# A routed expert layer: token table and gathers instead of scattered slots, and four result planes instead of two with accumulation

## The reference

```
logits = x2 @ gate_w.T
probs = jax.nn.softmax(logits, axis=-1)
top_w, top_i = jax.lax.top_k(probs, TOPK)           # 4 of 16 experts
top_w = top_w / jnp.sum(top_w, axis=-1, keepdims=True)
wfull = jnp.sum(jax.nn.one_hot(top_i, E, dtype=x2.dtype) * top_w[..., None], axis=1)
gu = jnp.einsum('th,eih->tei', x2, w1)              # 2 x 176 per expert
act = jax.nn.silu(g) * u
down = jnp.einsum('tei,ehi->teh', act, w2)
routed = jnp.einsum('te,teh->th', wfull, down)
shared = jax.nn.silu(sg) * su @ sh_down_w.T         # a dense expert of 352
return hid + (routed + shared).reshape(b, s, h)
```

## Time and profile before

| what | value |
|---|---|
| median of 3 runs | 1990.88 us (1988.37 to 1996.01) |
| the profiled execution's own time | 1989.11 us |
| its span in the profile | 1987.3 us |
| mean granted TensorE clock | 0.922 of full speed |
| busy share: PE, weight loads, DVE, ACT, POOL | 87%, 73%, 59%, 48%, 27% |
| `sort_and_share` | from 1609 us to 1756 us |
| `routed_experts`, first tile's load to last scatter landed | 1756 us to 1966 us |
| planes, adds, store | 1966 us to 1987 us |

### The profile page before, as it was taken

One profiled execution on the slowest core, in us unless ns is written; L12 is line 12 of the kernel. 1 busy time (PEld: TensorE's weight loads), 2 busy tenths in 40 slices (PEclk: granted clock), 3 DMA queues, 4 the chain that ended last, 5 costly groups with the idle time before them and its releaser, 6 DMA issues. The chain is left out here.

```text
span 1987.3 us, 34326 instructions
## 1 busy us (share of the span) xinstructions
PE 1722.4 (87%) x11668; PEld 1455.4 (73%) x11668; DVE 1165.0 (59%) x2625; ACT 951.5 (48%) x2452; POOL 529.5 (27%) x527
## 2 busy tenths in 40 slices
PE   7998897697699999999992999999999969259993
PEld 6666664555688888888881788888888867258883
DVE  4688884698655656566546555555555457335553
ACT  2577776486355444545541444444454423225442
POOL 4133321243311111111111111111121114736663
PEclk7699997898899999999996999999999968679997
DMA  4111121265100100100002101001000043447666
GB/s 142 55 34 29 29 70 40 78 252 213 43 13 1 43 12 13 43 1 11 1 1 77 43 1 32 12 12 29 5 12 1 1 117 108 147 101 139 126 115 162
DMA packets 73274, 117.40 MB, mean 59 GB/s; under 512 B 8285, under 2 KB 59021, under 8 KB 71943
## 3 DMA queue, kind: packets, MB, share of 16 engines
q1 hardware_dynamic: 54014, 89.03, 14.4%
q0 software_dynamic: 14448, 19.80, 5.6%
q10 hardware_dynamic: 4648, 6.38, 1.0%
HBM read 86.65 MB, written 44.70 MB: 66 GB/s over the span
## 5 line engine op out<-in xcount | busy, mean ns | idle before, releaser
L1812 ACT ACTIVATE da_prob<-da_prob,da_nb,d_rqs 128x128 f32<-128x128 f32 x256 | 123.3, 483 | 260.2 <-DVE da_nb L2072 260.2
L1812 ACT ACTIVATE hold_wq<-hold_wq,ca_nb,c_rqs 128x128 f32<-128x128 f32 x256 | 123.4, 483 | 235.4 <-DVE ca_nb L2072 235.4
L653 DVE TENSOR_REDUCE a_mx<-a_s 128x2 f32<-128x512 f32 x256 | 167.1, 681 | 60.5 <-PE a_s L541 58.7
L470 ACT ACTIVATE a_prob<-a_s 128x512 f32<-128x512 f32 x256 | 147.4, 600 | 85.7 <-PE a_s L554 85.4
L1874 POOL TENSOR_TENSOR hold_wq<-hold_wq,ca_rsum 128x512 f32<-128x512 f32 x64 | 66.7, 1042 | 428.3 <-DVE ca_rsum L2077 428.3
L1874 POOL TENSOR_TENSOR da_prob<-da_prob,da_rsum 128x512 f32<-128x512 f32 x64 | 66.6, 1041 | 422.9 <-DVE da_rsum L2077 422.9
L2700 POOL DMA_INDIRECT slot_results<-t_ysb,t_dest x79 | 124.3, 1574 | 91.7 <-ACT t_ysb L2714 42.8
L554 PE MATMUL a_s<-a_qs,a_ks 32*128 32x256 f32 x512 | 101.6, 346 | 32.4 <-ACT a_prob L470 32.3
L1884 PE MATMUL da_qk<-d_xTh,da_wqkv_h 128*128 128x512 f32 x256 | 106.7, 417 | 6.4 <-DVE da_wqkv_l L2023 6.4
L541 PE MATMUL a_s<-a_ks,a_qs 32*128 32x256 f32 x512 | 101.0, 351 | 3.1 <-DVE a_mx L653 3.0
L2084 DVE SCALAR_TENSOR_TENSOR ca_oT_l<-ca_oT,ca_bv,ca_oT_h 128x512 fp32r<-128x512 f32 x64 | 48.0, 751 | 93.3 <-ACT ca_oT_h L1826 93.3
(11 more groups left out here) (412 smaller groups left out, 5610.2 us busy)
## 6 DMA issues: line engine op xcount, KB each, us to landing
t_xg<-slot_rows SPq DMA_DIRECT2D x79, 144.0 KB, 2.5
mw_raw<-in_d_expert_w SPq DMA_DIRECT2D x16, 352.0 KB, 6.1
slot_results<-in_d_fill SPq DMA_DIRECT2D x1, 4608.0 KB
a_heads<-a_osb SPq DMA_DIRECT2D x128, 32.0 KB
a_wraw<-a_heads SPq DMA_DIRECT2D x32, 128.0 KB, 2.1
mw_down<-in_d_expert_d SPq DMA_DIRECT2D x1, 2816.0 KB
hold_wk<-in_c_wkT SPq DMA_DIRECT2D x1, 2064.0 KB
hold_wq<-in_c_wqT SPq DMA_DIRECT2D x1, 2064.0 KB, 9.0
```

The lines of the kernel that those rows point to most:

```text
L470: act.activation(prob[:, w % PR, :, :], s2[w % 2][:, :, :], ACT.Exp, scale=1.0 / A_ROOT)\
L653: dve.tensor_reduce(mx[:, b % 2, :, h], s1[s1_use(b, u) % S1_BANKS][:, :, :], AX.X, ALU.max)\
L1812: ins = act.activation(prob[:, p, b, :], prob[:, p, b, :], ACT.Exp, bias=nb[:, p, b:b + 1], scale=rqs[:, r:r + 1], accum_out=sums[:, p, b: ...
```

## The change

The slots are no longer filled by scattering rows. The 2048 token rows (272 numbers: token and weights of all experts) are stored once, by one plain DMA from SP, into a table `token_rows` in HBM. What a slot holds is found on chip: for each of 16 batches DVE builds one-hot matrices of the pair's lane within a tile (`in_lane`, 4 x 128 columns) and of its tile, multiplied by a label (`named`, 4 x 80 columns), in bfloat16 (`locate`). PE multiplies them into one PSUM tile (`find`, 4 matmuls a batch). The label's exponent holds batch and choice, its mantissa the token's lane, so the sum read as an integer is the token's number and choice; DVE turns it into two integer tables, `ids` and `dest` (`identify`). POOL then gathers each tile's 128 rows from `token_rows` with an indirect DMA into one of 44 row buffers. 28 gathers run in `sort_and_share`, 8 at the start of `routed_experts`, and 43 behind the scatters of the tiles.

The result rows of a tile go to the plane of the pair's choice (four planes). No token appears twice in a plane, so the scatter is plain and waits for no other. At the end 16 instead of 8 planes' groups are loaded, in eight buffers, and added. The two early fills are gone but for one row. Expert weights 5 to 8 are split within the shared units, as their places come free; the first five later than before (units 4 to 8 instead of 0 to 4).

```diff
-                sp.dma_start(slots.rearrange("(u r) n -> u r n", r=Y_BUFS * P), ...  # 11.8 MB
-                sp.dma_start(results.rearrange("(u r) n -> u r n", r=Y_BUFS * P), ...  # 4.7 MB
+                sp.dma_start(slots[0:1, :], fill[0:1, :]).then_inc(filled, 16)
...
+ROW = DIM + EXPERTS
+X_OWN, X_LOOSE = BATCHES, 16
+X_EARLY, X_AHEAD, X_BUFS = 28, 36, 44
+X_SEMS = 8
-PLANES = 2
+PLANES = 4
...
+    def gather(self, pool, slots, t, behind):
+        if t >= behind:
+            self.fetched(pool, t - behind)
+        pool.indirect_dma_start(self.tile(t), None, slots[:, :],
+                                bass.IndirectOffsetOnAxis(self.ids[:, t:t + 1], 0)).then_inc(self.x_in[t % X_SEMS], 16)
...
+                sp.wait_ge(meta_ready, 1)
+                sp.wait_ge(xn_ready, BATCHES)
+                sp.dma_start(slots[1:1 + BATCHES * TOKENS, :].rearrange("(b p) c -> p b c", p=P), rows[:, :, :])\
+                    .then_inc(rows_stored, 16)
...
-                for b in range(BATCHES):
-                    for k in range(TOPK):
-                        n = TOPK * b + k
-                        after(pool, sent_rows[n % IN_FLIGHT], 16 * (n // IN_FLIGHT))
-                        pool.indirect_dma_start(slots[:, :], bass.IndirectOffsetOnAxis(idx[:, b, k:k + 1], 0),
-                                                rows[:, b, :], None).then_inc(sent_rows[n % IN_FLIGHT], 16)
+                pool.wait_ge(ids_ready, 1)
+                for n in range(X_EARLY):
+                    first.gather(pool, slots, n, IN_FLIGHT)
...
+                def find(b):
+                    pe.wait_ge(lane_ready, b + 1)
+                    pe.wait_ge(named_ready, b + 1)
+                    for k in range(TOPK):
+                        mm = pe.matmul(f_ps, in_lane[:, b % DEEP, k, :], named[:, b % DEEP, k, :], ...
...
+                    if 1 <= t < 1 + GROUPS:
+                        find(GB * (t - 1))
+                        find(GB * (t - 1) + 1)
                     if t >= 2:
                         down(t - 2)
+                    if 1 <= t < 1 + GROUPS:
+                        find(GB * (t - 1) + 2)
+                        find(GB * (t - 1) + 3)
...
+                def locate(b):
+                    after(dve, found_psum, b - DEEP + 1)
+                    dve.tensor_tensor(in_lane[:, b % DEEP, :, :], lane_of[:, b, :].unsqueeze(2).broadcast_to([P, TOPK, P]),
+                                      lanes.unsqueeze(1).broadcast_to([P, TOPK, P]), ALU.is_equal).then_inc(lane_ready, 1)
+                    for k in range(TOPK):
+                        ins = dve.tensor_scalar(named[:, b % DEEP, k, :], times, tile_of[:, b, k:k + 1], cons[:, P + b + BATCHES * k:][:, 0:1],
+                                                ALU.is_equal, ALU.mult)
+                    ins.then_inc(named_ready, 1)
+                def identify():
+                    dve.wait_ge(found_psum, BATCHES)
+                    ...
+                    dve.scalar_tensor_tensor(first.ids[:, :], wanted[:, 1, :], -float(PLANE), wanted[:, 0, :],
+                                             ALU.mult, ALU.add).then_inc(ids_ready, 1)
...
-                    if t >= PLANES:
-                        pool.wait_ge(sent[(t - PLANES) % Y_BUFS], 16 * ((t - PLANES) // Y_BUFS + 1))
-                    d = t % D_BUFS
-                    pool.indirect_dma_start(results[:, :], bass.IndirectOffsetOnAxis(dest[:, d:d + 1], 0),
-                                            ysb[:, t % Y_BUFS, :], None, compute_op=ALU.add)\
-                        .then_inc(sent[t % Y_BUFS], 16)
+                    pool.indirect_dma_start(results[:, :], bass.IndirectOffsetOnAxis(first.dest[:, t:t + 1], 0),
+                                            ysb[:, t % Y_BUFS, :], None).then_inc(sent[t % Y_BUFS], 16)
+                    if t + X_AHEAD < NT:
+                        after(pool, xT_psum, t + X_AHEAD - X_BUFS + 1)
+                        after(pool, picked, t + X_AHEAD - X_BUFS + 1)
+                        first.gather(pool, slots, t + X_AHEAD, X_SEMS)
...
-                for n in range(GROUPS):
-                    load_plane(sp, n, 0)
+                for n in range(GROUPS):
+                    after(sp, added, PLANES * (n - 1))
+                    load_plane(sp, n, 0)
+                    load_plane(sp, n, 1)
+                    if n >= 1:
+                        store(n - 1)
...
                 for n in range(GROUPS):
-                    load_plane(act, n, 1)
+                    after(act, added, PLANES * (n - 1))
+                    load_plane(act, n, 2)
+                    load_plane(act, n, 3)
```

More of the change, by code:

```diff
@@ L2198, in __init__ @@
         self.pick = s.sb("pick", [P, TABLE, EXPERTS], BF16)
+        self.rows = s.sb("rows", [P, X_OWN, ROW])
+        self.loose = s.sb("loose", [P, X_LOOSE * ROW])
+        self.ids = s.sb("ids", [P, TABLE], mybir.dt.int32)
+        self.dest = s.sb("dest", [P, TABLE], mybir.dt.int32)
+        self.x_in = [s.sem(f"x_in{k}") for k in range(X_SEMS)]
         self.ld_d = s.sem("ld_d")
@@ L2294, in sort_and_share @@
         table_own = s.sem("table_own")
-        sent_rows = [s.sem(f"sent_rows{k}") for k in range(IN_FLIGHT)]
+        FREED = {n: -(-((n + 1 - EARLY) * 2 * W_COLS) // (2 * KT * GT)) for n in range(EARLY, SHARED)}
         def width(j):
@@ L2465, in _ @@
                         round_hid(t - 1)
+                    if EARLY + 2 <= t < SHARED + 2:
+                        n = t - 2
+                        act.wait_ge(u_psum, SH_TILES * FREED[n])
+                        first.split_hi(act, big, n)
                 round_hid(UNITS_S - 1)
                 act.wait_ge(acc_psum, UNITS_S)
-                for n in range(EARLY, EXPERTS):
+                for n in range(SHARED, EXPERTS):
                     first.split_hi(act, big, n)
@@ L2639, in routed_experts @@
         y_ps = [s.ps(f"y{k}", [P, 512]) for k in range(2)]
-        x_in = [s.sem(f"x_in{k}") for k in range(X_BUFS)]
         sent = [s.sem(f"sent{k}") for k in range(Y_BUFS)]
```

235 lines of the change are left out of this document (130 added, 105 removed).

## The result

The changed kernel took 2015.1 us (median of 7 runs, 2005.0 to 2019.3) against 1995.3 us before (7 runs, 1982.6 to 1999.2): a ratio of 1.0094, interval 1.0064 to 1.0124. It is slower by about 1%; the forecast was 1970 us and faster. The 1979.6 us of e15 in the table of experiments leave out one slow run of 2103.0 us.

The account below looks back on a forecast made before the run. POOL's descriptor making was taken to bound the first block, PE at 2.27 us a tile the tiles. Terms -25.9 - 4.3 - 5.0 + 14.1 = -21.1 took 1990.9 to 1970 us; own range 1963 to 1977, with rivals 1956 to 1986.

Parts of the forecast that it names:

- Term 1: From slot numbers to the first tile: POOL's gathers replace 64 scatters, first tile at 1732.4 instead of 1758.3 us, -25.9.
- Rival A: Cheaper at the seams: no landing at the border, gathers at 1.26 us, planes overlapping better; 1960 us, chance 0.20.
- rival C: A gather costs what the accumulating scatter costs, 1.85 us apart, stalling first block and tiles; +43, 2013 us, chance 0.07.
- Rival B: PE bounds the first one-hot units at the low clock, delaying `ids`; 1978 us, or 1986 with slower narrow instructions; chance 0.16.
- Term 2: In the tiles, accumulation's stalls of 5.3 us go, up to 1 us of POOL stall comes, PE stays 2.27 us apart; -4.3.
- term 3: From PE's last end to the plane loads: no queue of scatters behind one another (4.2 us); -5.0.
- The slack of 7.0 us: In the tiles, the margin before ACT's copy waits for the scatter four tiles back, shrinking to 0.1 us at tile 42.
- copies that wait for scatters between tiles 20 and 45: Sign in the tile loop listed as showing the forecast wrong; no size given.
- Term 4: The tail: four planes loaded, added and stored, 35.2 us from loads to end where it was 20.9; +14.1.
- Rival D: In the tiles, scatters queue behind gathers and land in 5 us, not 2.4; 1973 us, chance 0.52 together with the forecast.

Follow-up runs that it names:

- e15: The changed kernel with 36 row buffers and no gathers in the tile loop, like e1, beside e13; 1979.6 us, leaving out one slow run of 2103.0.
- e9: The changed kernel itself, word for word, run again in another job; 1987.5 us (10 runs, 1983.2 to 1998.1), without pauses.
- e13: The changed kernel a third time, unedited, as control of its job; 2016.9 us, with pauses.
- e16: The changed kernel with the scatters of tiles 0 to 35 issued after the last tile, gathers left in place; 2035.9 us.
- e2: The changed kernel with 7 arrival semaphores in place of 8, which also moves later semaphores' numbers by one; 1986.2 us, no pauses.
- e6: The changed kernel with 7 arrival semaphores and one unused one, keeping later numbers; paused, total time not given.
- e5: The changed kernel with 8 arrival semaphores and one unused one, moving later numbers by one; paused, total time not given.
- e10: The kernel of e2 (7 arrival semaphores) again, in the same job as e9; ratio 0.9967 against the kernel before.
- e17: The changed kernel without POOL's two semaphore waits ahead of each gather in the loop; paused, 5 us apart from e18.
- e11: The kernel of e1 (no gathers in the tile loop) again, in the same job as e9; its loop took 193.0 us.
- e1: The changed kernel with 36 row buffers and no gathers in the tile loop, so tiles 36 to 78 use old rows; 1978.1 us.
- job C: One set of kernels run one after another on one chip: e9 (1987.5 us), e10, e11 and a variant with plain loads for the loop's gathers.
- e18: The changed kernel itself once more, unedited, as control beside e17; 2022.4 us, with pauses.
- e14: The changed kernel without the eight gathers ahead of the first scatter, gathers spread over three tiles of four; 2010.3 us.

## Why the prediction was wrong

**Term 1 held** in its sum, -22.5 against -25.9 (-24.0 in e9), and partly by luck: `ids` 3.2 us late, the gathers' distance 4.0 us more in all, and a border 3.9 us shorter, outside its bounds. Rival A was right that nothing there waits for the last gather to land. The gather's price, the largest unknown, was chosen rightly: 0.97 us, so rival C fell. That the total of 2015 is near C's 2013 is chance. Rival B had the low clock right for the first units (0.64 and 0.68 granted from 1660 to 1680, 1.00 behind), but DVE was busy without a gap from 1670 to 1690, and PE was not what it waited for.

**Term 2 failed**, and with it the prediction: "DVE has one small instruction ...; the 2.27 us stand without a gap on PE. -4.3". What failed is that PE spaces the tiles without a gap. From the first tile to the last scatter it measured +23.8, where this term and the scatter queue's 4.2 of term 3 made -8.5. So it is 32.3 us off: 35.3 us in the two pieces below, less 3.0 by which the loop without either gained more than forecast.

- The pauses, 228.3 - 205.1 = 23.2 us (after against e9, the same program; 29 by e13). Some of it is the granted clock, 0.94 against 1.00 in the stretch shown, which fell where PE had idled. The sum had no term for them and none of the rivals had their form. I had bounded the price of a gather on the engine that issues it. I had not bounded what gathers do to the others, which no row of before could show, as there the tiles' rows came by plain loads. Shown is that the pauses in the tiles go when the gathers go (e15 has none after 1755.9; its last gather starts at 1753.4), that gathers alone 2.3 us apart don't bring them (e16), that they depend on the job (after, e9, e13), and that neither the semaphores (e2 with e6, e5, e10) nor the two waits of e17 make the difference. Not shown is the mechanism.
- POOL's pair. I had "up to 1 us of stall"; from the first tile to the last scatter it is 12.1 (e9 against e11; 9.4 by e2 against e1), of which 10.3 lie in the tiles with gathers. The slack of 7.0 us that shrinks to 0.1 was right in form and had nothing to spare for errors. The pair is 2.57 and not 2.52 (2.2 us over 43 tiles), an address batch gives 19.5 - 18.2 = 1.3 and not 1.8 (1.0 for two), and two scatters of e9 took 1.92 (at 1798.21) and 1.40 us instead of 0.99. These make 4.5 us. The landings, up to 4.1 us instead of 2.4, and the clock that PE loses by waiting are in the rest, which I have not divided. Where a slack comes out at 0.1, its error is the forecast. "copies that wait for scatters between tiles 20 and 45" stood in the text as what would make it wrong, and was seen in e9.

Without both the loop is 193.0 us, 11.5 less than before, where the 4.3 and the 4.2 make 8.5.

**Term 3 held**: -5.0 forecast, 3.2 against 8.25 us measured.

**Term 4** was 2.6 us too small: +16.7 against +14.1, near the +17 of its bound; 0.2 of that is a slip, as 35.2 less 20.9 is 14.3. The rate of 365 GB/s was right. What was too small is mainly the start, put at 1.6 us: DVE's first add waits 5.1 us behind the first issue for the first of eight loads that run side by side. e9 has the same 37.6 us.

So the sum from the save of `x_before` on is -22.5 + 23.8 + 15.6 = +16.9 in the execution shown, and -24.0 + 0.6 + 15.5 = -7.9 in e9. Without pauses the change is worth little: e9's ratio is 0.9983 (0.9958 to 1.0008), which can't be told from nothing, and the same kernel with seven semaphores has 0.9970 and 0.9967 (e2, e10), just clear of it. 15.5 us of tail and 12.1 in the loop eat most of the 24.0 of the first block and the 11.5 of accumulation. I had put 0.10 on no difference and 0.10 on slower, against 0.80 on faster; that was too sure, with a new kind of transfer in the loop that sets the time.

Rival D had the right outline (POOL moves the bound and the tiles don't follow), and gave 3 us where 10 were due. Its cause, landings of 5 us, is at most a part: in e9 the landings behind gathers that the trace has are 2.5 us in the median and 4.1 at most. What the early fills cost is not shown. The one trace of before has the save at 1051.24, and those of the changed kernel lie from 1047.6 to 1066.6 without the fills.

## What to carry to other kernels

Run the unedited kernel in every job. A one-digit edit looked like the cure by 29 us, and only the unedited kernel beside it in job C showed that it had done nothing.

Where an edit puts an operation that the trace lacks beside the loop that sets the time, bound its effect on that loop's other engines too, and not just its price where it is issued. Where one engine's slack comes out near zero, count it as a stall.

The time of a side engine's work is read over the stretch in which it stands, not over the loop: POOL has time to spare in the 79 tiles together, and none in the first 43.

## What the runs showed of the hardware

- PE's completions can be held back while the engine itself works on (e18: 9.9 us late at 1719.08, with matmuls until 1711.9). Among the tiles of jobs with pauses they came in bursts of four or five within 0.22 us. The time without a completion was within 0.1 us of 0.8, 1.5, 2.2, 2.9, 3.6 or 4.3 us, 0.7 apart, for nearly all bursts of after, e6, e13 and e14. About half of the bursts came 0.4 to 0.6 us after the first packet of a gather.
- Transfers were not slower for it. From the first tile on, packets of a gather took 208 ns in the median in after and 219 in e9, those of a scatter 179 and 178 ns.
- The same program took 2015.1, 1987.5, 2016.9 and 2022.4 us in four jobs, where the kernel before is level in the five of the table (medians 1993.5, 1993.7, 1993.0, 1991.8 and 1998.0 us). The runs of after and e9 do not touch.
